# A fused GNN layer and mixture of experts: the third part of the second aggregation in two column halves, biases after the second span, ranks of three kinds

## What is computed

```python
def gcn_conv(x, W, b, src, dst, n):
    h = x @ W.T
    deg = zeros(n).at[d].add(1.0);  dinv = deg ** -0.5        # s, d: edges and loops
    msg = h[s] * (dinv[s] * dinv[d])[:, None]
    return segment_sum(msg, d, n) + b
h = relu(gcn_conv(layernorm(x), W1, b1))                      # 1250 x 128
z = gcn_conv(h, W2, b2)                                       # 1250 x 64
x = x + (relu(relu(z @ Wd1.T + bd1) @ Wd2.T + bd2) @ Wd3.T + bd3)
xg = layernorm(x)[token_ids]                                  # sorted by expert
y[bin_ids == e] = gelu(xg @ w1[e]) @ w2[e]                    # for each of 8 experts
x = x + zeros.at[token_ids].add(w * y)
```

## Time and profile before

| | us |
|---|---|
| median of 3 runs | 179.66 |
| lowest, highest | 178.91, 180.84 |
| the profiled execution, its own time | 181.61 |
| its span, first to last instruction | 179.9 |

### The profile page before, as it was taken

One profiled execution on the slowest core, in us unless ns is written; L12 is line 12 of the kernel. 1 busy time (PEld: TensorE's weight loads), 2 busy tenths in 40 slices (PEclk: granted clock), 3 DMA queues, 4 the chain that ended last, 5 costly groups with the idle time before them and its releaser, 6 DMA issues.

```text
span 179.9 us, 3640 instructions
## 1 busy us (share of the span) xinstructions
PE 161.7 (90%) x1179; PEld 112.1 (62%) x1183; DVE 130.0 (72%) x297; ACT 93.3 (52%) x204; POOL 98.4 (55%) x74
## 2 busy tenths in 40 slices
PE   3689799999999999999999989999999999999900
PEld 1378677788898575586454444459777777768400
DVE  1899899999999699755843865967867856953300
ACT  3337677777786931233045376026778677545200
POOL 6089999999998000000018002874078887676632
PEclk9999999999999999999999999999999999999965
DMA  3995000000000499999000033448646656544581
GB/s 95 323 340 170 5 2 4 4 0 4 0 4 2 81 359 376 368 366 321 10 0 4 0 117 117 131 108 295 243 88 164 83 133 136 77 57 56 54 119 15
DMA packets 15546, 21.71 MB, mean 121 GB/s; under 512 B 3134, under 2 KB 8000, under 8 KB 15524
## 3 DMA queue, kind: packets, MB, share of 16 engines
q1 hardware_dynamic: 12994, 16.02, 26.6%
q0 software_dynamic: 2432, 5.24, 17.2%
q10 hardware_dynamic: 98, 0.17, 0.2%
HBM read 15.19 MB, written 6.23 MB: 119 GB/s over the span
## 4 chain that ended last, share of the span: by engine, by line
PE 71%; DVE 13%; POOL 7%; issue 3%; ACT 3%; POOLq 1%; ACTq 0%; DVEq 0%
PE bank L1584 15%; PE bank L1736 13%; DVE ring L724 8%; PE bank L1479 7%; PE bank L1708 7%; PE bank L1763 6%; PE bank L1747 4%; PE bank L1766 4%; PE bank L1454 3%; PE bank L1748 3%; POOL first_viol L617 3%; PE bank L1400 2%; DVE stats L1047 2%; DVE x_sb L1041 2%; PE bank L1444 1%
## 5 line engine op out<-in xcount | busy, mean ns | idle before, releaser
L635 POOL TENSOR_SCALAR_AFFINE_SELECT before<-ones_bf 128x128 bf16<-128x128 bf16 x1 | 37.8, 37836 | 0.0
L1479 PE MATMUL bank<-ring 128*128 128x110 bf16 x324 | 30.4, 229 | 4.8 <-DVE ring L724 4.0
L666 POOL DMA_INDIRECT out<-at,to_i x16 | 24.7, 1545 | 17.8 <-DVE at L1090 10.5
L1479 PEld LDWEIGHTS bank<-ring 128*128 128x128 bf16 x324 | 20.8, 102 | 11.9 <-issue 4.7
L724 DVE TENSOR_TENSOR ring<-iota_slots,lo 128x1024 bf16<-128x1024 f16 (+1 forms) x41 | 27.4, 668 | 0.0
L1193 ACT CAST at<-bank 128x400 f32 (+1 forms) x41 | 20.6, 504 | 10.5 <-PE bank L1485 8.5
L724 DVE TENSOR_TENSOR ring<-iota_dst,key 128x880 bf16<-128x880 f16 (+1 forms) x41 | 24.3, 593 | 0.0
L647 POOL CAST at_r<-ew 128x1024 fp32r<-128x1024 f32 x4 | 4.5, 1153 | 35.8 <-PE bank L1584 35.8
L1736 PE MATMUL bank<-at_r 128*128 128x512 f32 (+1 forms) x64 | 21.9, 406 | 0.0
L1022 DVE TENSOR_TENSOR ew_r<-ew,at_r 128x1024 fp32r<-128x1024 f32 x16 | 19.3, 1215 | 0.0
L1708 PE MATMUL bank<-wd3t_sb,at 128*128 128x512 f32 x40 | 18.0, 600 | 0.7 <-ACT at L1290 0.7
(11 more groups left out here) (209 smaller groups left out, 305.4 us busy)
## 6 DMA issues: line engine op xcount, KB each, us to landing
ew<-in_w SPq DMA_DIRECT2D x16, 512.0 KB, 9.4
x_sb<-in_x SPq DMA_DIRECT2D x9, 256.0 KB, 6.5
out<-x_sb SPq DMA_DIRECT2D x9, 256.0 KB, 4.5
wd3t_sb<-in_Wd3T SPq DMA_DIRECT2D x1, 512.0 KB, 4.9
x_rows<-xn SPq DMA_DIRECT2D x1, 512.0 KB, 2.8
x_rows<-at SPq DMA_DIRECT2D x1, 512.0 KB, 2.8
w1t_sb<-in_W1T SPq DMA_DIRECT2D x1, 256.0 KB, 6.2
bd_sb<-in_bd SPq DMA_DIRECT2D x1, 256.0 KB, 5.7
```

The lines of the kernel that those rows point to most:

```text
L635: nc.gpsimd.affine_select(out=before[:, :], in_=ones_bf[:, :], compare_op=ALU.is_gt, fill=0.0, base=0, pattern=[[1, P]], channel_multiplie ...
L666: nc.gpsimd.indirect_dma_start(out[0:T + 2 * SLOTS, :], bass.IndirectOffsetOnAxis(to_i[0:n, i, e:e + 1].bitcast(mybir.dt.uint32), 0), y_ou ...
L1479: last = mm(to, hot_src[:, j, t], hot_dst[:, j, t], start=(t == 0 and not ends), stop=(first and t == tiles - 1), skip_group_check=not ends)
```

## The change

1. The second aggregation. `part3` is 64 columns wide. The matmul of an even chunk writes rows 0 to 63 of the bank, that of an odd chunk rows 64 to 127, that is, each uses one half of the array's columns. Since the sums of both halves are added later, the result is the same. The padding and its semaphore are gone. The order is new: `part2` for chunks 0 to 8 of spans 0 and 1 only, then span 0's `part3` and chunk 9 of `part2`, the same for span 1, then span 2's `part2`, `decode1(0)`, and span 2's `part3`.
2. The four bias additions on DVE stand between the second `zt` and the third.
3. Ranks of three kinds: `late` as before, `early` (the token's other choice is the next expert, ranks from 0) and the others (ranks after the early ones). An early assignment is thus always in the 128 slots, so that the late ones in the 32 slots of expert e can share rows with the 128 slots of expert e-1 only. The add of 32 slots of expert e then waits only for the add of 128 slots of expert e-1, not for that of its 32; the adds of 32 have semaphores of their own, `s_added_more`. There is one more memset on POOL (8 columns), and the test of which path is taken has one more condition.

```diff
@@ POOL: adds to the output
-                    for i, n, ready, earlier in ((0, P, s_y, e - 2), (1, MORE, s_y_more, e - 1)):
-                        if earlier >= 0:
-                            pool.wait_ge(s_added[earlier % 2], 32 * (earlier // 2 + 1))
-                        pool.wait_ge(ready, e + 1)
+                    if e >= 2:
+                        pool.wait_ge(s_added[e % 2], 16 * (e // 2))
+                        pool.wait_ge(s_added_more[e % 2], 16 * (e // 2))
+                    pool.wait_ge(s_y, e + 1)
+                    add(0, P, s_added[e % 2])
+                    if e >= 1:
+                        pool.wait_ge(s_added[(e - 1) % 2], 16 * ((e - 1) // 2 + 1))
+                    pool.wait_ge(s_y_more, e + 1)
+                    add(1, MORE, s_added_more[e % 2])
@@ DVE: ranks
-            v.tensor_copy(loads[:, :, :], before_j[:, J])
-            route(v.tensor_tensor(ranks[:, :, :, :], chosen2[:, 0:J], before_j[:, 0:J], ALU.mult))
...
+            v.tensor_copy(first_rank[:, 0], before_j[:, J, 2])
+            v.tensor_copy(loads[:, :, :], before_j[:, J])
+            route(v.tensor_scalar(first_rank[:, 1], before_j[:, J, 1], -1.0, float(SLOTS), ALU.mult, ALU.add))
+            route(v.tensor_tensor(ranks[:, :, :, :], before_j[:, 0:J],
+                                  first_rank[:, :, :].unsqueeze(1).to_broadcast([P, J, KINDS, NE]), ALU.add))
+            v.tensor_tensor(loads[:, 0], loads[:, 0], loads[:, 1], ALU.add)
+            route(v.tensor_tensor(ranks[:, :, :, :], ranks[:, :, :, :], chosen_kind[:, 0:J], ALU.mult))
+            v.tensor_tensor(loads[:, 0], loads[:, 0], loads[:, 2], ALU.add)
+            route(v.tensor_reduce(rank[:, :], ranks[:, :, :, :].rearrange("p j h e -> p j (h e)"), AX.X, ALU.add))
@@ DVE: biases
-            add_bias(5, CH - 1)
             for i, (a, n) in enumerate(SPANS):
+                if i == len(SPANS) - 1:
+                    add_bias(5, CH - 1)
                 dve.wait_ge(s_agg2, i + 1)
@@ PE: second aggregation
+            def first_two_parts(s, spans):
+                wait_part2(0, s)
+                for i in spans:
+                    a, n = SPANS[i]
+                    last = mm(bank[4 + i][:, 0:n], part2[:, s], at[:, s, a:a + n], start=(s == 0), stop=(s == CH - 1))
+                return last
+            def finish_sums2(i):
+                a, n = SPANS[i]
+                for s in range(CH):
+                    wait_part2(1, s)
+                    half = s % 2 * LAT
+                    mm(bank[4 + i][half:half + LAT, 0:n], part3[:, s], at[:, s, a:a + n], start=False, stop=False,
+                       skip_group_check=True)
+                first_two_parts(CH - 1, (i,)).then_inc(s_agg2, 1)
+            for s in range(CH - 1):
+                last_product(s)
+                first_two_parts(s, (0, 1))
+            add_changes([part2, part3], wait_part2, (0, 1))
+            finish_sums2(0)
+            finish_sums2(1)
+            for s in range(CH - 1):
+                first_two_parts(s, (2,))
+            add_changes([part2, part3], wait_part2, (2,))
+            decode1(0)
+            finish_sums2(2)
             decode2(0)
```

More of the change, by code:

```diff
@@ L276, in gnn_moe @@
         chosen = sb("chosen", [P, J, NE], BF16)
[L277 to L280, removed]
+        KINDS = 3
+        chosen_kind = sb("chosen_kind", [P, J + 1, KINDS, NE], BF16)
+        in_turn = sb("in_turn", [P, TC, TOPK + 1])
+        paired = sb("paired", [P, TC, TOPK])
+        first_rank = sb("first_rank", [P, KINDS, NE])
+        ranks = sb("ranks", [P, J, KINDS, NE])
         rank = sb("rank", [P, J])
-        loads = sb("loads", [P, 2, NE])
-        load = sb("load", [P, 4])
+        loads = sb("loads", [P, KINDS, NE])
+        load = sb("load", [P, 6])
         path_i = sb("path_i", [1, 2], I32)
@@ L417, in gnn_moe @@
         s_added = [sem(f"s_added{i}") for i in range(2)]
+        s_added_more = [sem(f"s_added_more{i}") for i in range(2)]
         s_slots = sem("s_slots")
@@ L888, in _ @@
             link(v.tensor_tensor(repeats[:, :], gif[:, :, 0], gif[:, :, 1], ALU.is_equal))
-            for k in range(TOPK):
-                last = v.scalar_tensor_tensor(late[:, :, k], gif[:, :, 1 - k], 1.0, gif[:, :, k], ALU.add, ALU.is_equal)
+            for i, k in enumerate((0, 1, 0)):
+                v.scalar_tensor_tensor(in_turn[:, :, i], gif[:, :, 1 - k], 1.0, gif[:, :, k], ALU.add, ALU.is_equal)
             chosen_ck = chosen[:, :, :].rearrange("p (c k) e -> p c k e", k=TOPK)
@@ L1575, in spread_dinv, with add_changes, neighbours @@
                     last.then_inc(s_dinvT, 1)
-            def neighbours(parts, wait_part, done, after_pass, after_first=None, at_chunk=None):
+            def add_changes(parts, wait_part, spans):
+                with pe.If(slow != 0):
+                    for k in range(len(parts)):
+                        wait_part(k, CH - 1)
+                    with pe.Fori(0, CH) as s:
+                        for of in parts:
+                            m = of.shape[2]
+                            for i in spans:
+                                a, n = SPANS[i]
+                                mm(bank[4 + i][0:m, 0:n], of.rearrange("p c n -> p (c n)")[:, bass.ds(s * m, m)],
+                                   at2[:, :, :].rearrange("p c n -> p (c n)")[:, bass.ds(s * NP + a, n)],
+                                   start=False, stop=False, skip_group_check=True)
+            def neighbours(parts, wait_part, done, after_pass, after_first):
                 last_k = len(parts) - 1
@@ L1634, in rank_assignments @@
                 pe.wait_ge(s_chosen, 1)
-                wide = 2 * NE
-                mm(bank[7][:, 0:(J + 1) * wide], before[:, :], chosen2[:, :, :, :].rearrange("p j h e -> p (j h e)"),
+                wide = KINDS * NE
+                mm(bank[7][:, 0:(J + 1) * wide], before[:, :], chosen_kind[:, :, :, :].rearrange("p j h e -> p (j h e)"),
                    start=True, stop=False)
```

70 lines of the change are left out of this document (30 added, 40 removed).

## The result

| | kernel before | changed kernel |
|---|---|---|
| median, same chip | 180.82 us (20 runs) | 178.27 us (20 runs) |
| lowest to highest | 178.91 to 182.32 | 177.78 to 179.31 |
| ratio of the times | | 0.9871, interval 0.9852 to 0.9889 |
| profiled execution, its own time and span | 181.61, 179.9 | 178.07, 176.3 |

A forecast was written before the change was run, and what follows sets the result against it. PE bounds the kernel almost without a break from 60 us, then a tail of ACT and POOL's adds. The terms, -1.75 on PE and -1.4 in the tail, sum to -3.15: 179.66 - 3.15 = 176.5 us, range 175.3 to 179.2.

The forecast's parts named there:

- A: Second aggregation on PE: the third part's pairs run at once in two array halves; gains 2.70 us, bounds 0 and 2.70.
- B: Switching PE between wide and narrow matmuls, six times at 0.11 us: costs 0.6 us, bounds 0 and 1.3.
- bare loads: Rival (3): each of 30 narrow matmuls waits for its own load, 0.11 us each; 182.5 us, chance 0.07.
- C: New ranks, with more columns summed on PE and more steps on DVE: charged 0.2 us, range 0.15 to 0.7.
- D: New order of the second aggregation and its suppliers, with biases moved: costs 0.15 us, range 0 to 0.6.
- The two waits: At chunk 8 of the second aggregation: PE waits 0.1 us for ACT's hand-over and perhaps 0.1 for the branch.
- a sign of being wrong: The prediction is wrong if PE shows a wait on ACT or DVE before line 1727, the third-layer product.
- The sum on PE: Terms A to D together, up to the start of decode3(0): -2.70 + 0.6 + 0.2 + 0.15 = -1.75 us.
- E: Tail: POOL's last add starts 2.14 us earlier but lands in 3.8; gains 1.4 us, bounds 2.1 and -0.2.
- rival (1): The tail gives nothing: the last add is under way 5.4 us, only A to D count; 178.1 us, chance 0.20.
- Rival (4): A supplier is late: C's 0.7 and D's 0.6 hold; -2.2, 177.5 us; chance 0.62 together with the forecast.
- rival (2): The array halves take turns at the old pace: A is 0, B to D stay; -0.45, 179.2 us, chance 0.11.

## Why the prediction was right, point by point

**A (-2.70): right.** With one half in place of two the stretch grows by 2.53. The missing part lies at one seam: `decode2(0)` (line 1717) takes 1.98 us in the changed kernel and starts 0.18 behind the last wide matmul, with one half 1.88 and 0.12 (94.18 - 94.06), so some 0.16 of a wait for `y1` was hidden by the longer stretch. 2.53 + 0.16 = 2.69. That wait is real: ACT has `y1` at 90.43 + 0.69 = 91.12 us, and PE starts on it at 91.17.

By the rate in the Trainium skill (TensorE: Matmul & The Clock Gate, Part 3: Packing small matmuls) it would have been about 2.0, an estimate; that page's case is three tiles of 32 columns. Here two tiles of 64 gave the whole factor of 2, at 512 and at 256 columns.

**B (+0.6): right**, 0.66 measured between two kernels that differ in the width alone. The price was taken from the slot tables, with short matmuls; it is the same beside long ones, so it doesn't hide under them and doesn't grow with them. The way to the slower side (bare loads) isn't there: with all thirty in one half the pace stays 0.216 us, and the pairs keep the same pace.

**C (+0.2): too low, 0.34** between the first aggregation and the first chunk sum. The arithmetic of it was right: line 961 starts 72.82 - 59.61 = 13.21 us behind the first aggregation, line 945 before at 72.63 - 60.06 = 12.57, that is 0.64 late where 0.6 was forecast. The work of one PE stage more and DVE's lateness were taken as covering each other; they add up in part: counted from the first aggregation, the next group of its sums (line 1615) starts 8.13 us on, where it was 7.99, and the last 15.63, where it was 15.30. The range of C (0.15 to 0.7) held it.

**D (+0.15): right in size, not in what it is made of.** The stretch from the first chunk sum to `decode3(0)` fell by 1.95 us, and A, B and D as forecast make -1.95. With A and B as measured, D is 0.08. The two waits it was mainly made of aren't there. PE reaches chunk 8 at 83.14 + 8 x 0.216 = 84.87, just as ACT hands it over (84.55 + 0.30 = 84.85), and between the last wide matmul (85.12) and the first narrow one (85.43) there is room for one pace and one change of width, not for the branch. What is there is the 0.16 for `y1`, less 0.08 that the order gains. The biases are worth 1.6 (forecast: PE would wait 1.4), and only because of A, as the earlier trace rows had suggested. The 0.16 for `y1` is within the up to 0.2 named; it is a wait on ACT ahead of line 1727, which the prediction gave as a sign of being wrong, but a short one that it had priced.

**The sum on PE: -1.61** for -1.75, the difference being C.

**E (-1.4): right, 1.33** between four and ten profiles. It is the difference of two terms, as forecast: the last add starts 2.19 us behind the one ahead of it (mean of ten) in place of 4.04 (mean of four), 1.85 earlier where 2.14 was forecast, and then lands later, in 3.4 to 3.8 us (three profiles) in place of 3.0 or 3.1, where 3.8 was forecast. What was wrong is that nothing would be waited for: mostly a wait of 0.4 to 1.0 us for the 128-slot add takes the place of the 2 us or more. The first two profiles alone (9.86 and 8.31 us) would give 1.55.

**Where the 1.8 us between forecast and median come from.** By the median alone this forecast can't be called confirmed: 178.27 is nearer to the 178.1 of rival (1), the tail that gives nothing, than to 176.5. What decides against that rival are the tails of the traces and the run with the wait put back. The larger part of the 1.8 is the base: the forecast was set on 179.66, the median of three runs; twenty runs of the same kernel gave 180.82, 1.16 us higher. The other 0.6 is the gain, 2.55 between the medians (2.3 by the ratio, 2.0 to 2.7) for 3.15. That the result lies in the range is owed in part to its width. Its lower end was added up wrongly, too: 179.66 - 1.90 - 2.1 is 175.7, not 175.3. The sum was made against one execution, 181.61, which is 0.8 above the median of twenty, and whose last add waited longer than that of the second profile. By the stretches it is 1.61 on PE and 9.56 - 8.57 = 0.99 in the tail (means of the two profiles of before and the three of after), 2.6 in all, inside the interval. How long the tail waits in the unprofiled executions no run shows. The spread is no more than a hint: twenty executions of before lie within 3.4 us, of the changed kernel within 1.5.

**The rivals.** The tail that gives nothing, the halves that take turns and the bare loads are refuted, by the wait put back and by the kernel with one half. Rival (4), a late supplier, didn't come true: C is 0.34, D 0.08. The kernel with one half is what rival (2) described, and shows what B, C and D cost without A: from the first aggregation to `decode3(0)` 96.84 - 59.98 = 36.86 us, 0.93 more than before (0.95 forecast), of which the tail gives back 1.33. By the stretches it would be 0.4 faster than before, as rival (2) said; by the times that stays open.

## What to carry to other kernels

Two matmuls of 64 columns in the two halves of the array run as one, if they follow each other directly; going from full width to half and back costs 0.11 us each way, so that a group wants to be long, and narrow matmuls that stand together and end the sums save changes (four in place of six here). Work taken off the bounding engine is worth its length only if what the other engines do ahead of their next hand-over moves too: here 1.6 of 1.95 us hung on the place of four additions. Where a program ends on a chain of transfers, a wait that can be dropped by a proof that two writes can't meet can be worth nearly as much as the matmuls (here 1.33 us beside 1.61), and a forecast should be set on more than three runs.

## What the runs showed of the hardware

**An idle gap of PE, and the clock behind it.** All eight profiles from the first two chips show PE idle for 1.3 to 2.9 us at some place between 116 and 127 us, and then a lower granted clock; in the two with one half PE waits there for a gather, in the six others it is as in these rows. From `decode3(0)` to PE's last matmul these eight take 78.0 to 80.8 us, where the six others take 74.05 to 74.07. The first run with the wait put back, its windows (length, PE, PEld, DVE, ACT and POOL busy, granted clock, DMA share, GB/s) and the row of ACT behind the gap:

```profile
122.00:126.00 4.00, 1.92 (x12) 1.55 (x11) 2.21 (x4) 2.10 (x5) 0.05 (x1) 0.93 0.98 334
126.00:130.00 4.00, 4.00 (x12) 2.75 (x12) 3.05 (x6) 2.90 (x8) 0.00 (x0) 0.50 0.20 76
```

```profile
123.47 0.29 ACT L1365 COPY ring<-bank 128x160 f32<-128x160 f32 x1 [3.11 <-PE bank L1813]
```

PE had delivered at 121.1 (121.53 is the next group's start), yet ACT began at 123.47, and PE waited 2.08 us through DVE. Then the granted clock stood at 0.50, which is 1.2 GHz, for at least 4 us. From `decode3(0)` to PE's last matmul this profile takes 173.23 - 94.05 = 79.18 us, where the same kernel took 168.39 - 94.34 = 74.05 on the third chip: 2.08 us of idleness go with a loss of 5.1. The same place in the changed kernel's first profile has no gap and a clock of 1.00. What held ACT no view names; it is open. The kernel before is slower on these chips by as much, so it doesn't hang on the change, and it is why a stretch of a trace decided where medians could not.

**One instruction of GpSimd, short or very long.** The same instruction on the same data lasted 0.43, 4.36 and 37.9 us in three profiles, the first two of the changed kernel and the last of the kernel before:

```profile
16.04 0.43 POOL L639 TENSOR_SCALAR_AFFINE_SELECT before<-ones_bf 128x128 bf16<-128x128 bf16 x1
```

```profile
19.39 4.36 POOL L639 TENSOR_SCALAR_AFFINE_SELECT before<-ones_bf 128x128 bf16<-128x128 bf16 x1
```

```profile
19.34 37.87 POOL L635 TENSOR_SCALAR_AFFINE_SELECT before<-ones_bf 128x128 bf16<-128x128 bf16 x1
```

In the last DVE is busy without a break until 57.0, and the instruction ends at 57.2. The second ended when DVE had a gap, in a stretch in which the granted clock was lower and PE fed it late:

```profile
20.00:24.00 4.00, 3.62 (x26) 3.20 (x27) 3.60 (x7) 1.22 (x4) 3.80 (x2) 0.62 0.00 2
```

The Trainium skill (SBUF — State Buffer, Terms) describes a port pair that the two share and that one holds for a whole instruction. The two long rows fit that. The short one ran while DVE was just as busy, and DVE's instruction beside it took 0.70 us in place of 0.60; why GpSimd got its turn there and not in the others is open, and no run changed one of the two alone. How far the program's time hangs on it isn't shown either (the first aggregation starts at 59.61, 60.84 and 59.94 us in the three profiles). The large loads behind it do hang on it: in the changed kernel's first profile they run from 20 to 44 us, in the kernel before from 57 to 84.
